# Squared projections split into two parts in one 64-row operand: a block's norms as one fp32r product in place of an f32 one

## What is computed

```python
def reference(L0_attn_x, L0_attn_U, router_w, rg, ru, rd, sg, su, sd):   # names shortened
    x = L0_attn_x                                  # (4, 512, 128)
    xn = _layernorm(x, axis=-1)
    # attention by distance
    y = jnp.einsum('btd,dr->btr', xn, U)           # R = 32
    n = jnp.sum(y * y, axis=-1)
    cross = jnp.einsum('btr,bjr->btj', y, y)
    dist_sq = n[:, :, None] + n[:, None, :] - 2.0 * cross
    attn = jax.nn.softmax(-dist_sq, axis=-1)
    a = jnp.einsum('btj,bjd->btd', attn, xn)
    # feed-forward: a shared branch, and 8 experts of which each token uses 2
    shared = jax.nn.silu(xn @ sg) * (xn @ su) @ sd
    ...
    return x + a + shared + routed
```

## Time and profile before

| | before |
|---|---|
| time, median of 3 (lowest, highest) | 180.15 us (179.72, 181.58) |
| span of the profiled execution | 177.3 us |
| PE busy | 168.0 us, 95% |
| DVE busy | 101.1 us, 57% |
| ACT busy | 95.1 us, 54% |
| POOL busy | 83.1 us, 47% |
| products of `norms` (L988), in the chain | 4 times 0.95 us |

### The profile page before, as it was taken

How to read it: one execution, slowest core, us unless ns; L and a number is a source line. 1 busy time by engine, 2 the same in 40 slices (tenths; PEclk the granted TensorE clock), 3 DMA queues, 4 the chain that set the end, 5 groups by cost and what they waited for, 6 DMA issues and landing times.

```text
span 177.3 us, 3078 instructions
## 1 busy us (share of the span) xinstructions
PE 168.0 (95%) x1075; PEld 144.2 (81%) x1075; DVE 101.1 (57%) x246; ACT 95.1 (54%) x196; POOL 83.1 (47%) x89
## 2 busy tenths in 40 slices
PE   6798999999999999999999999999999999999970
PEld 6786766896799978888678899999998999888960
DVE  3997778999743746666987543242342432415484
ACT  2349967944789055557556455664655553344100
POOL 5230420004777777778450028768677683532000
PEclk9999999999999999999999999999999999999996
DMA  5999999800111111000473006364472100101994
GB/s 166 310 196 155 267 282 334 253 6 15 63 48 59 39 51 31 5 0 0 86 247 118 0 0 183 107 220 113 142 240 71 37 18 22 37 15 32 297 284 122
DMA packets 29117, 20.72 MB, mean 117 GB/s; under 512 B 2253, under 2 KB 25832, under 8 KB 29104
## 3 DMA queue, kind: packets, MB, share of 16 engines
q1 hardware_dynamic: 27312, 17.89, 37.9%
q0 software_dynamic: 1792, 2.65, 4.7%
HBM read 12.36 MB, written 7.92 MB: 114 GB/s over the span
## 4 chain that ended last, share of the span: by engine, by line
PE 68%; DVE 10%; ACT 7%; DMA 7%; SPq 4%; issue 2%; POOLq 1%; DVEq 0%; POOL 0%
PE bank L1147 13%; PE bank L939 12%; PE bank L941 9%; PE bank L940 9%; PE bank L1015 8%; DVE yR L797 5%; PE bank L1059 4%; ACT yL L490 4%; DVE silu L791 4%; DMA row<-routed_dram 3%; SPq L325 3%; DMA sw_raw<-in_L_ffn_su_dram 3%; PE bank L988 2%; PE bank L1000 2%; PE bank L1127 2%
## 5 line engine op out<-in xcount | busy, mean ns | idle before, releaser
L482 ACT ACTIVATE silu<-bank 128x512 f32<-128x512 f32 (+1 forms) x64 | 33.1, 517 | 29.9 <-PE bank L941 29.8
L394 POOL DMA_INDIRECT slots_dram<-row,slot_i x32 | 32.6, 1018 | 27.5 <-issue 27.5
L791 DVE TENSOR_TENSOR hid_e<-bank,silu 128x320 f32<-128x320 f32 x32 | 15.7, 491 | 35.1 <-ACT silu L482 35.1
L400 POOL TENSOR_TENSOR ew_lo<-ew_raw,ew_hi 128x1024 fp32r<-128x1024 f32 x8 | 19.1, 2383 | 22.3 <-ACT ew_hi L504 22.3
L408 POOL DMA_INDIRECT routed_dram<-eo,xg x24 | 23.0, 960 | 13.1 <-ACT eo L518 7.1
L939 PE MATMUL bank<-xnT_hi,sw_hi 128*128 128x512 f32 x64 | 26.1, 408 | 0.5 <-ACT silu L482 0.5
L941 PE MATMUL bank<-xnT_hi,sw_lo 128*128 128x512 f32 x64 | 25.1, 393 | 0.0
L940 PE MATMUL bank<-xnT_lo,sw_hi 128*128 128x512 f32 x64 | 25.0, 391 | 0.0
L1147 PE MATMUL bank<-rd,hid_e 128*128 128x128 f32 (+1 forms) x192 | 23.7, 276 | 0.0
L1147 PEld LDWEIGHTS bank<-rd,hid_e 128*128 128x128 f32 (+1 forms) x192 | 22.0, 173 | 1.0
L939 PE MATMUL bank<-xgT_hi,ew_hi 128*128 128x320 f32 x64 | 21.1, 330 | 0.0
(11 more groups left out here) (146 smaller groups left out, 264.9 us busy)
## 6 DMA issues: line engine op xcount, KB each, us to landing
ew_raw<-in_L_ffn_rg_dram SPq DMA_DIRECT2D x8, 256.0 KB, 2.9
ew_raw<-in_L_ffn_ru_dram SPq DMA_DIRECT2D x8, 256.0 KB, 3.1
rd<-in_L_ffn_rd_dram SPq DMA_DIRECT2D x8, 256.0 KB, 2.9
routed_dram<-fill SPq DMA_DIRECT2D x1, 2048.0 KB, 12.4
row<-routed_dram SPq DMA_DIRECT2D x8, 256.0 KB, 4.7
slots_dram<-fill SPq DMA_DIRECT2D x1, 1300.0 KB, 13.2
xg<-slots_dram SPq DMA_DIRECT2D x8, 130.0 KB, 2.9
acc<-in_L_attn_x_dram SPq DMA_DIRECT2D x4, 256.0 KB, 4.0
```

Of the source, the lines that this page charges most:

```text
L394: G.indirect_dma_start(slots_dram, bass.IndirectOffsetOnAxis(slot_i[:, k, t:t + 1], 0), row[:, t, 0:RW], None, bounds_check=E * CAP - 1, o ...
L400: G.tensor_tensor(ew_lo[:, e % 2, :, :], ew_raw[:, e % 2, :, :], ew_hi[:, e % 2, :, :].bitcast(F32), ALU.subtract).then_inc(ew_ready, 1)
L482: C.activation(silu[:, q % 2, 0:n], gate_b[q % 2][:, 0:n], ACT.Silu).then_inc(silu_ready, 1)
L791: V.tensor_tensor(hid, up_b[q % 2][:, 0:n], silu[:, q % 2, 0:n], ALU.mult).then_inc(hid_ready, 1)
```

## The change

The squares are no longer summed in f32. ACT squares 64 rows of the bank (two of the three copies of y) with a result rounded to fp32r, into `ysq_parts`. It squares the second copy once more in f32, into `ysq`. DVE subtracts the one from the other in rows 32 to 63, which leaves the rest of the rounding there. One fp32r product over the 64 rows then sums high parts and rests. Its weights `minus_half` are 128 columns wide, zero but for four columns of -0.5, so that it writes all 128 rows of the bank. It waits for DVE's subtraction (`ysq_split`), and for both subtractions of `y_lo(g)` (`y_parts_ready`), since these read what it writes over. The squares stand ahead of the two copies in `y_hi`.

```diff
-        half = sb("half", [R, 4])
+        minus_half = sb("minus_half", [2 * R, P], F32R)
...
-        ysq = sb("ysq", [R, T])
+        ysq = sb("ysq", [2 * R, 2, S])
+        ysq_parts = sb("ysq_parts", [2 * R, 2, S], F32R)
...
                 act.wait_ge(y_done, g + 1)
+                if g >= 2:
+                    act.wait_ge(n_done, g - 1)
+                C.activation(ysq_parts[:, g % 2, :], turn_b[g % 2][0:2 * R, :], ACT.Square)
+                C.activation(ysq[R:2 * R, g % 2, :], turn_b[g % 2][R:2 * R, :], ACT.Square).then_inc(ysq_ready, 1)
                 C.copy(yL[0:3 * R, cols], turn_b[g % 2][0:3 * R, :])
                 C.copy(yR[0:3 * R, cols], turn_b[g % 2][0:3 * R, :]).then_inc(y_hi_s, 1)
-                C.activation(ysq[:, cols], turn_b[g % 2][0:R, :], ACT.Square).then_inc(ysq_ready, 1)
...
-            V.memset(half[:, :], -0.5)
+            V.memset(minus_half[:, :].bitcast(F32), 0.0).then_inc(halves_set, 1)
+            dve.wait_ge(halves_set, 1)
+            V.memset(minus_half[:, NR].bitcast(F32), -0.5).then_inc(halves_set, 1)
...
                 ps = turn_b[g % 2]
+                dve.wait_ge(ysq_ready, g + 1)
+                V.tensor_tensor(ysq_parts[R:2 * R, g % 2, :], ysq[R:2 * R, g % 2, :],
+                                ysq_parts[R:2 * R, g % 2, :].bitcast(F32), ALU.subtract).then_inc(ysq_split, 1)
                 dve.wait_ge(y_hi_s, g + 1)
...
                 V.tensor_tensor(yL[2 * R:3 * R, cols], ps[2 * R:3 * R, :],
-                                yR[2 * R:3 * R, cols].bitcast(F32), ALU.subtract)
+                                yR[2 * R:3 * R, cols].bitcast(F32), ALU.subtract).then_inc(y_parts_ready, 1)
...
-                pe.wait_ge(ysq_ready, g + 1)
-                M(turn_b[g % 2][NR, :], half[:, :], ysq[:, S * g:S * g + S], start=True, stop=True
+                if g == 0:
+                    pe.wait_ge(halves_set, 2)
+                pe.wait_ge(y_parts_ready, g + 1)
+                pe.wait_ge(ysq_split, g + 1)
+                M(turn_b[g % 2][:, :], minus_half[:, :], ysq_parts[:, g % 2, :], start=True, stop=True
                   ).then_inc(n_done, 1)
```

More of the change, by code:

```diff
@@ L238, in moe_attention_kernel @@
         ysq_ready, n_done, nhi_ready = sem("ysq_ready"), sem("n_done"), sem("nhi_ready")
+        halves_set, ysq_split, y_parts_ready = sem("halves_set"), sem("ysq_split"), sem("y_parts_ready")
         norm_split, yL_ready = sem("norm_split"), sem("yL_ready")
```

## The result

The changed kernel takes 193.02 us (median of 4, 192.85 to 193.72) against 179.96 us. The ratio is 1.071 (95% interval 1.065 to 1.077). The forecast was 189.7 us, with a range up to 192.8. The direction was right and the time lies 0.2 us above the range: what came is the second rival, the clock that falls twice.

A forecast was written before the change was run, and what follows sets the result against it. PE was taken to bound the attention stage. Stalls of 11.25 us less 3.7 saved give +7.55, +7.05 without the 0.5 us wait for experts' rows; with 2.5 for the clock, 180.15 becomes 189.7 us, range 186.8 to 192.8.

The forecast's parts named there:

- the second rival: The clock falls a second time, at the 2.85 us stall ahead of norms(2): +1.6 us, 191.3 us; chance 0.35.
- The saving on PE: In the attention, the new product and the matmul behind it take 0.23 us each: 0.92 us saved, four times 3.7.
- behind a break: Upper bound for the new product on PE: 0.43 us, against 0.23 in a stream; saving then 0.72 us each, 2.9 altogether.
- ACT's squares: On ACT ahead of the copies in y_hi: one more square adds 0.48 us, so y_hi_s comes 0.96 us later.
- norms(0): First new product on PE: stands 0.75 us until y_lo(0) ends on DVE, against 0.92 us saved.
- norms(1): Second new product on PE: stands 6.75 us, since y_lo(1) is behind sel in DVE's list and ends at 36.9 us.
- norms(2): Third new product on PE: stands 2.85 us for DVE's block sum (0.73 us) and three subtractions (2.1 us).
- norms(3): Fourth new product on PE: there after 3.65 us, y_lo(3) ends at 4.55, so it stands 0.9 us.
- The clock: PE restarts at 1.2 GHz after the 6.75 us stall, low for 5.0 us, costing 2.5 us; own case's chance 0.42.
- Nothing gives back, nothing is added behind: After the attention nothing gives much back; only PE's 0.5 us wait for the experts' rows goes: +7.55 becomes +7.05 us.
- What lies around the span: Profiled span 177.3 us against the median of 180.15: 2.85 us lie around the span.
- The other side: Rival: no stall at norms(1), y_lo(1) ending before 30.2 us: +0.8 us, or 178.1 us; chance 0.02 for under 1% slower.

The follow-up runs named there:

- both fillings: Changed kernel with 85 products of ones on PE ahead of norms(1) and 35 ahead of norms(2), all waits kept: 188.80 us.
- e5: Changed kernel with y_lo(1) moved forward in DVE's list, from behind sel to behind chunk 5's multiplication: 187.68 us, ratio 1.044.
- the work alone: Kernel before plus the added square and subtraction, f32 product kept and waiting for the squares alone: 180.70 us, ratio 1.005.
- the first filling: Changed kernel with 85 products of ones on PE ahead of norms(1) only, all waits kept: ratio 1.051, executions 188.30 to 194.46 us.
- the wait alone: Kernel before, f32 product and one square kept, with only norms(g) waiting for both subtractions of y_lo(g): 192.63 us, ratio 1.068.

## Why the prediction was right or wrong

- **PE bounds the stage; a stall is lost.** Right. The stretches before and after add up to the loss at the end of the attention, and nothing came back behind it.
- **The sums.** Two slips: 0.92 saved less 0.75 of stall is 0.17 us, not 0.1; and the lower end of the forecast's own range is 189.7 - 0.5 - 1.4 = 187.8, not 188.2. Neither decides anything.
- **The saving on PE.** The mechanism is right, the size was wrong. The product costs 0.40 us and the matmul behind it 0.34 us (26.53, 26.93, 27.27), near the bound "behind a break" and not the 0.23 I took. Before, the two took 24.95 to 26.23 on the same scale of starts, 1.28 us, so each saves 1.28 - 0.74 = 0.54 us, 2.2 us in all, not 3.7. At `norms(3)` there was no wait, and the product still took 0.42 us of the chain; why it is never as short as one in a stream no run shows.
- **ACT's squares.** I took 0.48 us for a step. Between squares it is 0.60:

```profile
22.73 0.59 ACT L453 ACTIVATE ysq_parts<-bank 64x512 fp32r<-64x512 f32 x1
23.33 0.59 ACT L454 ACTIVATE ysq<-bank 32x512 f32<-32x512 f32 x1
23.94 0.58 ACT L455 CAST yL<-bank 96x512 fp32r<-96x512 f32 x1
```

  PE stood 26.53 - 25.49 = 1.04 us there, not 0.75. With the smaller saving this is what made `norms(0)` cost 0.42 us where I had a small gain.
- **DVE's subtraction.** 0.68 to 0.78 us, 0.70 taken.
- **`norms(1)`.** 6.75 us forecast, 37.67 - 31.23 = 6.44 measured.
- **`norms(2)`.** 2.85 forecast, 52.85 - 49.95 = 2.90 measured.
- **`norms(3)`.** 0.9 forecast for full clock; 1.08 with both fillings. In the changed kernel it is nothing, since PE came there at half clock, as the second rival said.
- **The clock.** The first fall came: 2.5 us forecast, 2.16 measured. The step that failed is the choice between one fall and two, 0.42 against 0.35. The second fall cost 1.99 us (1.6 in the rival's sum). I had the end of the span in front of me, where it had fallen 2.4 us after the last product, and still gave a wait of 2.85 us less than even chances.
- **Nothing gives back, nothing is added behind.** The first scatter came at 50.8 us (50 forecast), and I took 0.5 us off for PE's wait for the experts' rows. That wait is gone, but in the wide stage PE waits longer ahead of the product that reads DVE's rests (L1112). Weight loads first, then products (us, times, longest):

```profile
PEld bank L1112 <- issue: 1.6, 2, 1.1
```

```profile
PE bank L1112 <- DVE yR L807: 0.7, 1, 0.7
```

  Before, the products had 0.4 us of this in two waits. The 0.7 us end with a DVE step that takes 0.69 us elsewhere and lies beside a step of POOL of 93.81 to 96.25 us:

```profile
94.25 2.56 DVE L807 TENSOR_TENSOR yR<-silu,yL 128x512 fp32r<-128x512 f32 x1 [0.69 <-ACT yL L495]
```

  So behind the attention 0.6 us were added.
- **What lies around the span.** I took 2.85 us, the difference of a profiled span and a median. The runs show 1.7 us (193.72 and 192.0 for the changed kernel); the profiled execution of before was one of the shorter ones.
- **The sum.** The spans were to differ by 9.55 us and differ by 14.7. Of the 5.1 us between, the clock has 1.65 (4.15 instead of 2.5), the product 1.5 (2.2 saved instead of 3.7), the part behind the attention 1.1 (0.6 added instead of 0.5 taken off), the start 0.6 and the stalls 0.1 (0.96 + 6.44 + 2.90 + 1.08 = 11.38 with the clock up, instead of 11.25); 0.2 us stay open. By the medians the kernels are 13.1 us apart and not 14.7, since the profiled execution of before was a short one and that of after the longest. That is 3.5 us more than forecast, and 3.3 in the time, since the kernel before took 179.96 us and not 180.15.
- **The other side.** That the wait ahead of `norms(1)` would be absent was rightly given next to nothing.

## What to carry to other kernels

A cheaper instruction that needs more inputs should be priced by the latest of them: look up where the last producer stands in its engine's list, not how long it takes. Where an in-order engine bounds the stage, add to each new wait of a few microseconds the work done at half clock behind it; here two waits of 9.3 us cost 4.2 us more. Moving the wait's producer forward won 5 us with one step, but what stood in its place comes later, and others wait for that in turn: after the best rearrangement tried, the change was still 2% slower.

## What was not expected of the hardware

The clock fell after far less idle time than the 6.4 us. In the changed kernel it had fallen while PE stood for 2.9 us; in e5 behind two waits of under 1 us each. In the profiled execution of the work alone, of 182.03 us, it fell at 90.5 us, behind the wait for the experts' rows, in which PE's products stood 1.7 us:

```profile
90.00:92.00 2.00, 2.00 (x7) 1.51 (x7) 1.46 (x1) 0.00 (x0) 0.91 (x1) 0.62 0.85 289
```

And a gap of the same length does not always do it. Behind the warming PE stands until ACT's first rows are there, 1.03 us in the trace of before. In the changed kernel it stood 2.25 us there and in the first filling 2.55 us, since the first weights landed at 7.48 and 8.26 us instead of 6.98. The changed kernel kept its clock, as did the work alone with 2.67 us. In the first filling the clock fell near 9.3 us, while PE stood:

```profile
9.40:12.40 3.00, 2.57 (x18) 2.25 (x19) 2.21 (x10) 1.83 (x7) 0.86 (x1) 0.50 1.22 232
```

There it stayed at half until 16.15 us; with both fillings (2.50 us of idle time) from 9.4 to 12.8, and with the wait alone (2.46 us) from 9.5 to 13.0. These profiled executions are the slowest of their kernels, 194.46, 190.02 and 195.49 us, so the later weights and the low clock together are the likely reason for part of the spread. Of the 2 us by which the profiled execution of the wait alone lies late, 1.2 are there before the low clock can cost anything (9.73 against 8.55 us at the product behind the gap). The kernel before, too, has single executions of 181.4 to 183.2 us among those of 179.1 to 179.7; that they are these has not been shown.

The other is the kind of chip on which the engines stand still while the scatters run. The waits of ACT, of the work alone there (us, times, longest):

```profile
ACT hid_s L479 <- remote: 34.5, 1, 34.5
```

What it waits for, the trace does not say.
